# A state-space image network on one core: layer 1's sequences prepared in pairs of 384 columns with the taps on ScalarE and VectorE, and the other layers' preparation in pairs

## What is computed

```
xc = conv_general_dilated(xs, conv_w, (1,), [(D_CONV - 1, 0)], feature_group_count=D_INNER)   # 4 taps, along the sequence
xc = silu(xc + conv_b)                                                    # u
dt, Bm, Cm = split(einsum('nld,ed->nle', xc, x_proj_w), ...)              # B, C, 6 rows of dt
delta = softplus(einsum('nlr,dr->nld', dt, dt_proj_w) + dt_proj_b)        # delta
h = exp(delta * A) * h + (delta * u) * B;   y = h . C + u * D             # the scan, not touched
```

## Time and profile before

| | us |
|---|---|
| median of 3 runs (32547.73 to 32561.99) | 32549.22 |
| the profiled execution | 32541.78 |
| its span in the trace | 32540.0 |
| busy: PE / DVE / POOL / ACT | 25162.3 / 25022.1 / 22360.7 / 14914.3 |

### The profile page before, as it was taken

How to read it: one execution, slowest core, us unless ns; L and a number is a source line. 1 busy time by engine, 2 the same in 40 slices (tenths; PEclk the granted TensorE clock), 3 DMA queues, 4 the chain that set the end, 5 groups by cost and what they waited for, 6 DMA issues and landing times. The chain is left out here.

```text
span 32540.0 us, 337692 instructions
## 1 busy us (share of the span) xinstructions
PE 25162.3 (77%) x99334; PEld 7908.5 (24%) x99334; DVE 25022.1 (77%) x16153; ACT 14914.3 (46%) x20317; POOL 22360.7 (69%) x10001
## 2 busy tenths in 40 slices
PE   6877888887446778888887778888883778888885
PEld 3432222221113322222222322222221322222222
DVE  1248999999421259999996469999995469999996
ACT  1035555554233345555550345555552345555552
POOL 0017999998000059999995149999992049999992
PEclk8867888888757778888885768888886768888887
DMA  2033222222312222222226342222225332222224
GB/s 72 10 134 78 51 43 51 43 51 83 116 39 109 96 78 43 51 43 51 43 45 221 137 127 47 47 45 49 43 51 173 141 120 51 43 51 43 50 44 162
DMA packets 1094283, 2419.75 MB, mean 74 GB/s; under 512 B 117178, under 2 KB 574719, under 8 KB 1082981
## 3 DMA queue, kind: packets, MB, share of 16 engines
q1 hardware_dynamic: 1092524, 2398.69, 26.7%
HBM read 1375.26 MB, written 1023.05 MB: 74 GB/s over the span
## 5 line engine op out<-in xcount | busy, mean ns | idle before, releaser
L1307 POOL TENSOR_TENSOR scan_hc<-scan_bc,scan_h 128x1024 f32<-128x1024 f32 x6912 | 16092.3, 2366 | 108.6 <-DVE scan_h L1471 107.5
L1471 DVE TENSOR_TENSOR_SCAN scan_h<-scan_da,scan_state,scan_dbu 128x1024 f32<-128x1024 f32 x6912 | 15992.5, 2339 | 137.6 <-ACT scan_da L1359 132.0
L1390 PE MATMUL scan_da<-scan_dd,scan_ssel 32*128 32x512 f32 x27648 | 9101.0, 745 | 3012.8 <-DVE scan_h L1471 2780.8
L1359 ACT ACTIVATE scan_da<-scan_da,scan_a_cur 128x1024 f32<-128x1024 f32 x6912 | 7516.1, 1087 | 7724.6 <-PE scan_da L1390 7717.3
L1390 PE MATMUL scan_p_du<-scan_dd,scan_ssel 32*128 32x512 f32 x27648 | 9200.1, 745 | 532.9 <-DMA scan_bc<-bc_d 218.4
L1458 DVE TENSOR_TENSOR scan_dbu<-scan_p_du,scan_bc 128x1024 f32<-128x1024 f32 x4608 | 5565.5, 1208 | 508.5 <-PE scan_p_du L1390 475.1
L1293 POOL TENSOR_TENSOR scan_dbu<-scan_bc,scan_dus 128x1024 f32<-128x1024 f32 x2304 | 5455.3, 2368 | 146.3 <-ACT scan_dus L1333 145.7
L1390 PEld LDWEIGHTS scan_da<-scan_dd,scan_ssel 32*128 32x128 f32 x27648 | 2450.2, 216 | 10295.1 <-DVE scan_h L1471 8735.0
L1407 PE MATMUL scan_p_y<-scan_hc,scan_rsel 128*32 128x512 f32 x27648 | 4775.3, 772 | 17.0 <-POOL scan_hc L1307 16.2
L1390 PEld LDWEIGHTS scan_p_du<-scan_dd,scan_ssel 32*128 32x128 f32 x27648 | 2410.7, 211 | 3622.1 <-DVE scan_dbu L1458 2970.7
L1338 ACT ACTIVATE scan_state<-scan_h,scan_a_cur 128x1 f32<-128x1 f32 x6912 | 2023.4, 293 | 1583.9 <-DVE scan_h L1471 1476.2
(11 more groups left out here) (216 smaller groups left out, 15630.3 us busy)
## 6 DMA issues: line engine op xcount, KB each, us to landing
scan_bc<-bc_d SPq DMA_DIRECT2D x576, 512.0 KB, 12.1
delta_d<-prep_delta SPq DMA_DIRECT2D x384, 576.0 KB, 4.5
scan_dd<-delta_d SPq DMA_DIRECT2D x1152, 192.0 KB, 4.8
scan_dd<-du_d SPq DMA_DIRECT2D x1152, 192.0 KB, 6.7
y_d<-scan_y SPq DMA_DIRECT2D x576, 384.0 KB, 5.2
merge_y<-y_d SPq DMA_DIRECT2D x384, 576.0 KB, 5.7
du_d<-prep_useq SPq DMA_DIRECT2D x288, 576.0 KB, 4.7
xs_d<-proj_xs_o SPq DMA_DIRECT2D x96, 588.0 KB, 3.3
```

What stands on the lines that cost most here:

```text
L1307: nc.gpsimd.tensor_tensor(hc[:, u % HC_SLOTS, :], c, h[:, u % H_SLOTS, :], ALU.mult).then_inc(hc_ready, 1)
L1359: nc.scalar.activation(da[u % DELTA_BANKS][:], da[u % DELTA_BANKS][:], ACT.Exp, scale=a_cur[:, slot(u)[0], u % UNITS:u % UNITS + 1]).then_ ...
L1390: return nc.tensor.matmul(dst[:, half * H:(half + 1) * H], ssel[rows, i, :], dd[rows, s, m, j, :], start=True, stop=True)
L1471: nc.vector.tensor_tensor_scan(h[:, v % H_SLOTS, :], da[v % DELTA_BANKS][:], dbu[:, v % DBU_SLOTS, :], state[:, v % UNITS:v % UNITS + 1], ...
```

## The change

In `prepare` nothing is added or taken away, only the order within a pair of steps changes: PE expands both steps and then projects both; DVE multiplies the pair's first step with u before the next pair's two caps and the second behind them; SP stores delta as soon as it is ready (but in layer 0), ahead of du.

`prepare_causal` is new. It runs 48 turns over pairs of 384-column steps (768 columns), with no loop instruction. In turn i PE expands pair i+1 and projects pair i+2, while pair i+3 is convolved and pair i+4 copied. PE no longer convolves: ACT does the last tap with the bias (`first_tap`), DVE adds the other three (`add_taps`), one instruction of 128x768 per tap and tile, and ACT applies silu to all three tiles at once (128x2304). du moves to POOL (`times_u`). There are four slots of `useq`, four of `dtv`, three of `delta`, and still one `raw`. Cap, Exp, Ln and softplus work on 128x1152 as in `prepare`. Weights are loaded for one direction, since all are the same. The diff, cut to its core:

```diff
@@ -792,17 +792,30 @@
                     sp.wait_ge(dtv_ready, v + 1 + ONE)
                     sp.dma_start(bc_d[:, v * N:(v + 1) * N], dtv[0:BC_ROWS, v % DTV_SLOTS, :]).then_inc(bc_stored[v % DTV_SLOTS], 16)
+                def store_du(v):
+                    sp.wait_ge(du_ready, v + 1 + ONE)
+                    sp.dma_start(du_d[:, :, v * N:(v + 1) * N], piece(v)).then_inc(du_stored[v // PIECES % SLOTS], 16)
+                def store_delta(v):
+                    if l == 0:
+                        sp.wait_ge(reset_done, v + 1 + ONE)
+                    else:
+                        sp.wait_ge(delta_ready, v + 1 + ONE)
+                    sp.dma_start(delta_d[:, :, v * N:(v + 1) * N], delta[:, v % SLOTS]).then_inc(delta_stored[v % SLOTS], 16)
                 for v in range(2):
                     store_bc(v)
-                for v in range(STEPS):
-                    if v + 2 < STEPS:
-                        store_bc(v + 2)
-                    sp.wait_ge(du_ready, v + 1 + ONE)
-                    sp.dma_start(du_d[:, :, v * N:(v + 1) * N], piece(v)).then_inc(du_stored[v // PIECES % SLOTS], 16)
-                    if l == 0:
-                        sp.wait_ge(reset_done, v + 1 + ONE)
-                    sp.dma_start(delta_d[:, :, v * N:(v + 1) * N], delta[:, v % SLOTS]).then_inc(delta_stored[v % SLOTS], 16)
+                for v in range(0, STEPS, 2):
+                    for b in range(2):
+                        if l != 0:
+                            store_delta(v + b)
+                        if v + b + 2 < STEPS:
+                            store_bc(v + b + 2)
+                    for b in range(2):
+                        store_du(v + b)
+                        if l == 0:
+                            store_delta(v + b)
@@ -846,10 +859,12 @@
                 t.wait_ge(loaded, 16 * 4 + ONE)
                 for v in range(2):
                     project(v)
-                for v in range(STEPS):
-                    expand(v)
-                    if v + 2 < STEPS:
-                        project(v + 2)
+                for v in range(0, STEPS, 2):
+                    for b in range(2):
+                        expand(v + b)
+                    for b in range(2):
+                        if v + b + 2 < STEPS:
+                            project(v + b + 2)
@@ -902,244 +917,277 @@
                     for b in range(2):
                         softplus(v + b)
                     for b in range(2):
-                        if v + b + 2 < STEPS:
-                            cap(v + b + 2)
-                    for b in range(2):
                         times_u(v + b)
                         if l == 0:
                             reset(v + b)
+                        if b == 0:
+                            for c in range(2):
+                                if v + c + 2 < STEPS:
+                                    cap(v + c + 2)
...
 def prepare_causal(nc, l, w, map_d, map_cols, delta_d, du_d, bc_d, useq_d):
...
+        N = SUB
+        PAIR = 2
+        MAJ = 8
+        DW = MAJ * SIDE
+        PER = SIDE // MAJ
+        PAIRS = DIRS * PER
+        STEPS = PAIRS * PAIR
+        SLOTS = 4
+        DELTA_SLOTS = 3
+        DTV_SLOTS = 4
+        AHEAD = 4
+        MULTS = SEQ_TAPS - 1
...
+                def store_u(j):
+                    sp.wait_ge(useq_ready, j + 1 + ONE)
+                    sp.dma_start(useq_d[:, :, j * DW:(j + 1) * DW], useq[:, j % SLOTS]).then_inc(useq_stored[j % SLOTS], 16)
...
+                for i in range(-AHEAD, PAIRS):
+                    if pair(i):
+                        for b in range(PAIR):
+                            store_delta(i * PAIR + b)
+                        for b in range(PAIR):
+                            store_du(i * PAIR + b)
+                    if pair(i + 2):
+                        for b in range(PAIR):
+                            store_bc((i + 2) * PAIR + b)
+                    if pair(i + 3):
+                        store_u(i + 3)
...
             @block.gpsimd
+                def times_u(v):
+                    g.wait_ge(delta_ready, v + 1 + ONE)
+                    g.wait_ge(useq_stored[v // PAIR % SLOTS], 16 * (v // PAIR // SLOTS + 1) + ONE)
+                    g.wait_ge(dbl_done, v + 1 + ONE)
+                    g.tensor_tensor(piece(v), delta[:, v % DELTA_SLOTS], piece(v), ALU.mult).then_inc(du_ready, 1)
+                def walk_tile(j, m):
+                    if j == 0:
+                        g.wait_ge(grid_loaded[m], 16 + ONE)
+                    g.wait_ge(tapped[m], j * MULTS + ONE)
+                    g.wait_ge(first_ready, max((j - 1) * TILES + m + 1, 0) + ONE)
+                    if j % PER == 0:
+                        g.memset(raw[:, m, 0:HALO], 0.0).then_inc(halo_ready, 1)
+                    else:
+                        g.tensor_copy(raw[:, m, 0:HALO], raw[:, m, DW:DW + HALO]).then_inc(halo_ready, 1)
+                    g.wait_ge(halo_ready, j * TILES + m + 1 + ONE)
+                    dst, src = walk(j, m)
+                    g.tensor_copy(dst, src).then_inc(raw_ready, 1)
+                for i in range(-AHEAD, PAIRS):
+                    if pair(i):
+                        for b in range(PAIR):
+                            times_u(i * PAIR + b)
+                    if pair(i + 4):
+                        for m in range(TILES):
+                            walk_tile(i + 4, m)
...
             @block.tensor
+                def project(v):
+                    t.wait_ge(useq_ready, v // PAIR + 1 + ONE)
+                    t.wait_ge(dtv_ready, max(v - 1, 0) + ONE)
+                    for m in range(TILES):
+                        last = nc.tensor.matmul(p_dbl[v % 2][:, 0:N], wx[:, m, :], piece(v)[:, m, :], start=(m == 0), stop=(m == 2))
+                    last.then_inc(dbl_done, 1)
+                def expand(v):
+                    t.wait_ge(dtv_ready, v + 1 + ONE)
+                    t.wait_ge(delta_ready, max(v - 1, 0) + ONE)
+                    for m in range(TILES):
+                        q = DT_ROWS[m % 2]
+                        last = nc.tensor.matmul(p_dt[v % 2][:, m, 0:N], wdt[q:q + K, m, :], dtv[q:q + K, v % DTV_SLOTS, :],
+                                                start=True, stop=True)
+                    last.then_inc(dt_done, 1)
+                t.wait_ge(loaded, 16 * 6 + ONE)
+                for i in range(-AHEAD, PAIRS):
+                    for b in range(PAIR):
+                        if pair(i + 1):
+                            expand((i + 1) * PAIR + b)
+                    for b in range(PAIR):
+                        if pair(i + 2):
+                            project((i + 2) * PAIR + b)
...
             @block.scalar
+                def first_tap(j, m):
+                    a.wait_ge(raw_ready, j * TILES + m + 1 + ONE)
+                    a.wait_ge(du_stored[j % SLOTS], 16 * PAIR * (j // SLOTS) + ONE)
+                    nc.scalar.activation(useq[:, j % SLOTS, m, :], raw[:, m, HALO:HALO + DW], ACT.Identity, bias=conv_b[:, m:m + 1],
+                                         scale=tapv[:, m, SEQ_TAPS - 1:SEQ_TAPS]).then_inc(first_ready, 1)
+                def silu(j):
+                    for m in range(TILES):
+                        a.wait_ge(tapped[m], (j + 1) * MULTS + ONE)
+                    nc.scalar.activation(useq[:, j % SLOTS], useq[:, j % SLOTS], ACT.Silu).then_inc(useq_ready, 1)
+                def take(v):
+                    a.wait_ge(dbl_done, v + 1 + ONE)
+                    a.wait_ge(dt_done, max(v - DTV_SLOTS + 1, 0) + ONE)
+                    a.wait_ge(bc_stored[v % DTV_SLOTS], 16 * (v // DTV_SLOTS) + ONE)
+                    nc.scalar.activation(dtv[:, v % DTV_SLOTS, :], p_dbl[v % 2][:, 0:N], ACT.Identity, bias=ones[:]).then_inc(dtv_ready, 1)
+                a.wait_ge(loaded, 16 * 6 + ONE)
+                for i in range(-AHEAD, PAIRS):
+                    if pair(i + 1):
+                        for v in range((i + 1) * PAIR, (i + 2) * PAIR):
+                            a.wait_ge(capped, v + 1 + ONE)
+                            nc.scalar.activation(sp_b[:, v % PAIR], sp_b[:, v % PAIR], ACT.Exp).then_inc(exp_done, 1)
+                        for v in range((i + 1) * PAIR, (i + 2) * PAIR):
+                            a.wait_ge(exp_done, v + 1 + ONE)
+                            nc.scalar.activation(sp_b[:, v % PAIR], sp_b[:, v % PAIR], ACT.Ln, bias=1.0).then_inc(log_done, 1)
+                    if pair(i + 4):
+                        first_tap(i + 4, 0)
+                    if pair(i + 2):
+                        for b in range(PAIR):
+                            take((i + 2) * PAIR + b)
+                    if pair(i + 3):
+                        silu(i + 3)
+                    if pair(i + 4):
+                        for m in range(1, TILES):
+                            first_tap(i + 4, m)
...
             @block.vector
+                def add_taps(j, m):
+                    own = useq[:, j % SLOTS, m, :]
```

(27 more changed lines are left out.)

249 lines of the change are left out of this document (68 added, 181 removed).

## The result

| | before | after |
|---|---|---|
| median, us | 32549.9 (32547.73 to 32561.99, 4 runs) | 30852.38 (30842.74 to 30871.03, 4 runs) |
| span of the profiled execution | 32540.0 | 30853.3 |
| mean granted clock | 0.806 | 0.821 |

The changed kernel takes 0.9478 of the time of before, 95% interval [0.9462, 0.9495]. The forecast was 30991 within 30700 to 31480.

What follows compares the result with a forecast made beforehand. PE was taken as the busiest engine, its projection inside the loop of layers 0, 2 and 3 and its convolution filling layer 1. Savings of 642 and 909 us from 32541.8 gave 30991, range 30700 to 31480.

Steps and rivals of the forecast that it cites:

- PE fast throughout: Rival for layers 0, 2 and 3: PE always at the high clock, turn 10.5 us, 113 us less than forecast; chance 6%.
- 520 to 550 us named: Sign of being right: softplus in each of layers 0, 2 and 3 lies within 520 to 550 us.
- A clock near 0.7: Sign of being right: PE's granted clock in layers 0, 2 and 3 is near 0.7.
- SP's order at nothing: Layers 0, 2 and 3: SP's reordering of the stores was costed at nothing.
- 0.9 of the 1.02: Layer 1: each DVE tap holds POOL off and is held off by it for 0.9 of its 1.02 us.
- in the last three a halo and a copy come between: Layer 1's turn: its last three taps are delayed by POOL copies, ending at 19.4 us (rows) or 20.9 (columns).
- Taps with a median over 1.1: Sign of being right in layer 1: DVE's taps have a median over 1.1 us and a tail to 3.
- left even: Layer 1's start: no gain from loads, since the map comes tile by tile but the first silu needs all three.
- port no limit: Rival for layer 1: DVE and POOL don't hinder each other, ACT bounds a 15.6 us turn, 203 us less; chance 12%.
- nothing overlaps: Rival for layer 1: none of POOL's 9.3 us overlaps DVE's 14.95, turn 24.2 us, 185 us more; chance 13%.
- PE stays at the low clock: Rival for layers 0, 2 and 3: low clock keeps the turn at 14.1 us, 395 us more than forecast; chance 17%.
- the two of the wrong sign: Rivals: taps wait behind long POOL instructions, 32634 us; or waits serialise layer 1's turns, about 32540 us; 1% each.

## Why the prediction was right, point by point

Both terms of the sum were too small, by 73 and by 63 us, and in the same direction: no error of one made up for the other, and the 139 us between forecast and median are their sum with 3 us between executions.

**That layers 0, 2 and 3 gain by PE's order: right, and shown** by undoing it. The term was mis-sized: 642 us predicted, 715 measured, turn 11.3 against 10.8. The step that was off is the clock. I let PE spend 11.2 of a turn, projections 6.8 and expansions 4.4, and gave the loop 11.1 on that account. In the fast turn above the two expansions take 2.84 in one piece, and the two projections 5.83: 8.7, and over the phase 9.0 (3.6 and 5.5 in layer 3's window). So PE has slack, and the "PE fast throughout" case, which I gave 6%, describes the loop in such a turn: DVE and ACT set it. My 10.5 for that case was too long by 0.4, because I counted a pair on DVE as 2.75 (measured 2.53 from start to start, 2.62 with its end) and a product as 1.31 (1.27). What lies between 10.1 and the 10.9 of layer 3 is products that meet a POOL copy (the pair's first product, the one ahead of the caps, has a mean of 1.71 in that window against 1.35 undisturbed, 0.4 a turn; the second is off the path) and DVE's waits for an expansion (15.3 us in 45 turns, 0.3), in the turns where PE is at the low level. The 0.2 I took for the former was the right thing at about half its size (in layer 0 it is 0.2). So the phases lie just under the 520 to 550 us named.

"A clock near 0.7" was wrong: 0.80. The reason against PE staying slow, was sound; what I had not seen is that in more than half of the turns both expansions, not a part of them, run at the high level. The rule of the Trainium skill, page "TensorE: Matmul & The Clock Gate", section "What you observe", that sustained matmuls release the throttle, is borne out by the run with every projection doubled (0.96) more plainly than by the changed kernel.

**DVE's order in these layers: inside the sum, but not weighed.** I treated the product ahead of the caps as part of DVE's chain but did not ask what the loop would be without it. It lies on the path, and in layers 2 and 3 that part of the change costs some 31 and 26 us. In layer 0 it saves 35, by letting delta's store go earlier, a wait that I had not named.

**SP's order at nothing: right** for the changed kernel, as far as the spread of the runs lets one tell.

**Layer 1, 909 predicted, 972 measured.** From POOL's first instruction to last store's issue it is 929.4 us (9631.25 to 10560.69) where I had 970:

| part | predicted | measured |
|---|---|---|
| POOL's start to first softplus | 33 | 53.0 |
| 45 full turns | 904.5 | 850.8 |
| two turns without taps | 24.4 | 21.6 |
| rest | 8.5 | 4.1 |
| loads, against before | 0 | -25.6 |
| last store to the scan's first load, against before | 0 | 2.6 |

The turn is 18.9 in the mean in place of 20.1 (under the 19 to 21 named), and its structure is the one forecast: DVE the bound, columns longer (19.56) than rows (18.19), the taps behind softplus in a tug with POOL's products. By its steps for a row turn, from softplus: 2.75, 6.65, 2.7 and 7.3 predicted; 2.53, 6.61, 2.53 and 6.52 measured. So the exclusion, "0.9 of the 1.02", was good to 0.05 us in a row direction and to 0.2 in a column direction (7.35 predicted, 7.19 measured); what failed is the last step, "in the last three a halo and a copy come between". I charged those with all of POOL's time, 0.95 and 1.75. In the rows above six taps cost 0.4 more than six alone (6.12), and in a column direction 1.2. A further 0.4 is the pairs on DVE, as in the other layers.

"Taps with a median over 1.1" was wrong with it: the median is 1.019, since six of nine taps meet little; the mean, 1.515, shows the stretch. "Products lengthened to over 3 us" holds for some (maximum 3.36, mean 2.96, median 2.65). The maximum of a tap, 3.26, fits the "tail to 3". How layer 1's gain divides among the parts of its new form (no convolution on PE, pairs, more slots) no run tells: the runs vary only where du is computed.

The loads were "left even", and the start of the copies was not. The layer's start in the timeline, in the kernel before:

```profile
9844.95 0.55 SPq L396 DMA_DIRECT2D z_d<-proj_z_o  x1
...
9892.40 0.11 POOL L1011 MEMSET prep_halo<- 128x9 f32 x1 [345.89 <-DMA prep_grid<-xs_d]
```

and in the changed one:

```profile
9609.03 0.54 SPq L396 DMA_DIRECT2D z_d<-proj_z_o  x1
...
9631.25 0.10 POOL L1069 MEMSET prep_raw<- 128x3 f32 x1 [321.10 <-DMA prep_grid<-xs_d]
...
9644.62 0.10 POOL L1069 MEMSET prep_raw<- 128x3 f32 x1 [12.39 <-DMA prep_grid<-xs_d]
...
9655.73 0.10 POOL L1069 MEMSET prep_raw<- 128x3 f32 x1 [10.12 <-DMA prep_grid<-xs_d]
```

Before, POOL began 47.5 us after the last store of the phase ahead, when the whole map was there. Now it begins after 22.2, with the first tile, and then waits for the others, 12.4 and 10.1 us. The whole map is there after 46.7 us (9655.73), hardly earlier than before. So the 25.6 gained ahead of the first copy are mostly given back behind it, in the 20.0 by which the lead is longer than I had it. The two errors of the ledger belong together and leave 5.6.

**The exclusion on the port** (rival "port no limit", 12%): its premise fell. With the products all but gone three taps take 3.11, with them 7.27. The Trainium skill, page "SBUF — State Buffer", section "SBUF: two separate sides", has the loser blocked for the whole instruction; three taps alone (3.06) and two products alone (5.2) make 8.3, and measured from the first product's start to the last tap's end it is 7.8 in both kinds of direction, so near the sum, with 0.5 overlapped. Of the three taps it is the first two that are long (2.92 and 3.26 in a column direction), one for each product; the third takes 1.02. By the Trainium skill, page "GPSIMD Engine Reference", section "Performance versus the Vector engine", that elementwise work belongs on DVE, layer 1 would be faster with du there. By 43 us it was. I set that rule aside because DVE, the bound, is rid of 2.7. The rule was the better guide: a pair of products moved to POOL came back to DVE as 3.6 us of stretched taps in rows and 4.2 in columns, where DVE's own work on them is 2.5 from start to start.

**The other rivals**: "nothing overlaps" (24.2 a turn), "PE stays at the low clock" (14.1) and the two of the wrong sign did not come; the first in part because two of POOL's three walk copies in a turn fall beside softplus and caps, which have an operand in `p_dt`, in PSUM, and are not held up: at 9730.18 a copy beside the caps takes 0.82, as short as any.

## What to carry to other kernels

PE may be slow because of how its work lies in time: putting its short pieces together took it from 12.7 to 9.0 us a turn for the same instructions, and its projections out of the loop besides. Work moved off the bounding engine onto one that gets in its way was not got rid of here: count what it takes from the bound's own instructions (here 3.6 to 4.2 us a turn against 2.5), and place it beside instructions that don't compete. And when an order is changed, ask per phase which store hangs on it; the same three lines cost some 30 us in each of two layers and saved 35 in the third, and one more slot had both.

## What the runs showed that was not expected

The level of PE's clock does not follow the kind of matmul here. In the fast turn of layer 3 above, the expansions with 13 of 128 rows run at the high level (2.84 us for two, granted clock 1.00) although PE was idle for 0.8 us just before them, and those of the next turn do so after 1.5 us. The first matmuls of the projections behind them run at the low one. The weight loads of these projections, from the same timeline:

```profile
24613.90 0.34 PEld L845 LDWEIGHTS prep_p_dbl<-prep_useq,prep_wx 128*128 128x128 f32 x1 [0.23 <-issue]
24614.54 0.34 PEld L845 LDWEIGHTS prep_p_dbl<-prep_useq,prep_wx 128*128 128x128 f32 x1 [0.30 <-issue]
...
24617.10 0.85 PEld L845 LDWEIGHTS prep_p_dbl<-prep_useq,prep_wx 128*128 128x128 f32 x3 [0.30 <-issue]
```

They stand 0.64 us apart at first, and the last three take 0.85 together; the granted clock is 0.65 from 24612.73 to 24615.90, and 1.00 again in the 1.5 us without work behind 24618.56. So the level comes late in both directions: what a matmul is granted goes back to what PE did some time before it. These runs don't tell more of it than that.

A copy of three columns on POOL is busy 0.92 us where it takes 0.19 alone, when it starts under a tap that is under way; and the same pair of products beside taps costs 4.2 us in a column direction and 3.6 in a row direction, where the walk copy ahead of it ends earlier, so that the first product begins 1.1 us ahead of the first tap (9722.07 against 9723.18) and not 0.5 (10007.15 against 10007.68).
